# Two layers of a fused graph network: ScalarE's one-hot casts behind the link copies, and layer two's row products three slots ahead

## The chip, the cores and the metric

The kernel runs on one core of one Trainium2 chip. The metric is the device time of one launch in microseconds, as the median of several runs. Three runs of the kernel before took 2488.91, 2496.96 and 2488.14 us; the median is 2488.91.

## What is computed

Three graph attention layers over 3125 nodes with 256 features and 53,125 edges sorted by destination, with a residual and a layer norm behind the second and behind the third. The first two layers have four heads and one head; the third has eight and adds edge features to the scores. The first two add one more loop from each node to itself. Cut to what matters:

```python
def gat_layer(x, src, dst, W, a_src, a_dst, bias, heads, out_ch):
    xW = (x @ W).reshape(n, heads, out_ch)
    alpha_s, alpha_d = jnp.sum(xW * a_src, axis=-1), jnp.sum(xW * a_dst, axis=-1)
    e = leaky_relu(alpha_s[src] + alpha_d[dst], 0.2)
    m = segment_max(e, dst)
    w = jnp.exp(e - m[dst])
    alpha = w / segment_sum(w, dst)[dst]
    return segment_sum(xW[src] * alpha[:, :, None], dst).reshape(n, -1) + bias

h = elu(gat_layer(x, ...,  heads=4, out_ch=64))       # layer one
x = layernorm(x + gat_layer(h, ..., heads=1, out_ch=256))   # layer two
x = layernorm(x + third_layer(x, edge_attr_3, ..., heads=8, out_ch=32))   # layer three
```

## The kernel before

**Batches and slots.** The sorted edges are cut into tiles of 128. A tile that touches two blocks of 128 nodes counts twice, so there are 440 slots; a batch is 11 slots (`B`), and each layer runs 40 batches (`K`). The program is written out batch after batch by `batches(eng, period)`; each engine has its own `period(t, left)` that goes through the slots s = 0 to 10 of batch t and, between them, does pieces of the work for later batches: for the next (`n1`), the one after (`n2`) and the third (`n3`). Each layer's table `AT` says at which slot which piece stands; it is the order of the work, written by hand. Engines meet only by semaphores, and each works its own list strictly in order.

**The work of one batch.** The names are those of the code; the lines are of the profile.

- GpSimd (POOL) fetches the rows of the source nodes with one indirect DMA a slot (L1271) into `rows`, a ring of three batches. The fetches of batch t+3 reuse the buffers of batch t, so slots 0 to 3 wait until the sum of slot 3 of batch t is done, slots 4 to 7 for the sum of slot 7, slots 8 to 10 for the last.
- VectorE makes `onehotT`, the one-hot form of each tile's destinations (`hot`, L716). TensorE transposes it, slots 0 to 5 as group 0 and 6 to 10 as group 1, into banks 0 and 7 (`hot` on PE, L1696, at slots `hotP`). ScalarE casts each group to the float tile `onehot` (`hotT` on ScalarE, L1433, at the two slots `AT[l]["hotT"]`): 128x768 and 128x640. These are the casts of the change. They wait for the transposes and for the sums of the batch two before.
- Scores: TensorE fetches the destination terms (`adst`, L1709), VectorE adds (`scores`, L730 to L742), TensorE transposes (`scoresT`, L1726), ScalarE copies (`scores`, L1440), VectorE scans for the maximum of each segment in both directions (`tops`, L758, `tops2`, L766).
- Links across slots: TensorE turns the ends of the rows (`endsT`, L1735 to L1739), VectorE scans them (`links`, L776, L778, L785), ScalarE copies them to `linkrow` (`link`, L1449, L1450) and computes the factor for older sums (`rescale`, L1457, L1460), TensorE turns the copies to columns (`cols`, L1746) and the factor (L1755), VectorE finishes the maxima (`finish_tops`, L792 to L800).
- Weights: ScalarE takes the exponential (`expw`, L1466), VectorE masks (L808), TensorE transposes (`weightsT`, L1763, L1766), ScalarE copies the weights to `wgt` (L1472, L1474).
- Row products: each slot's rows are multiplied by its weights, on VectorE (L828) or on ScalarE (L1481, one instruction a head), as `OWNER` says. In layer one ScalarE has slots 0, 2, 3, 5, 6, 8 and 9; in layer two all but slot 0. An engine makes the product of slot s + `LEAD[l]` at slot s, running over into the next batch.
- Sums: TensorE multiplies `onehot` with the products (`sum_slot`, L1775, two passes a slot), and VectorE adds the result into `sums` (`add`, L839), after rescaling (L820) at the start of a batch.

**The order around the change.** On TensorE, slot s of the first two layers is the sum of slot s, and behind it the pieces of that slot: in layer one the one-hot groups at 1 and 2, ends at 2, columns at 4, destination terms at 6, weights at 7, scores at 9; in layer two one-hot groups at 0 and 1, ends at 1, columns at 4, destination terms at 5, weights at 7, scores at 8. On ScalarE a slot is written so:

```python
for s in range(B):
    if left > 1:
        if s == AT[l]["link"]:
            link(n1)
            rescale(n1)
        ...
    if s + LEAD[l] in OWN[l]["A"]:
        mul(t, s + LEAD[l])
    if left > 1 and s + LEAD[l] - B in OWN[l]["A"]:
        mul(n1, s + LEAD[l] - B)
    if left > 2 and s in AT[l]["hotT"]:
        hotT(n2, AT[l]["hotT"].index(s))
```

Of the kernel before, what the change touches and what calls it, by code (L numbers as in the profile page):

```python
# [63 lines left out]

OWNER = ("AVAAVAAVAAV", "VAAAAAAAAAA", "VAVAPAPAPAP")
OWN = tuple({e: tuple(s for s in range(B) if o[s] == e) for e in "VAP"} for o in OWNER)
LEAD = (3, 2, 2)
TROW = 8
XPART = 4
PAIRS = (BLOCKS + 1) // 2  # L70
# [13 lines left out]

AT = (
    dict(tops2=1, links=3, finish=5, mask=6, scores=7, tops=10, hot=4, load=5,
         link=5, exp=7, weights=8, hotT=(3, 4), copy=8,
         endsT=2, cols=4, weightsT=7, hotP=(1, 2), adst=6, scoresT=9),
    dict(tops2=0, links=1, finish=5, mask=6, scores=7, tops=10, hot=3, load=8,
         link=2, exp=7, weights=7, hotT=(0, 1), copy=7,  # L90
         endsT=1, cols=4, weightsT=7, hotP=(0, 1), adst=5, scoresT=8),
    dict(links=2, finish=5, mask=10, scores=5, tops=10, hot=7, load=7,
         link=3, exp=6, weights=8, hotT=(2, 6), copy=9,
# [23 lines left out]
def gat_kernel(nc, x, src, dst, edge_attr, w1, as1, ad1, b1, w2, as2, ad2, b2, w3, as3, ad3, edge_w, edge_b, b3, out):  # L117
    ctx = ExitStack()
    with ctx:
# [292 lines left out]
        def _(dve):  # L412
# [247 lines left out]
            for l in range(3):  # L660
# [142 lines left out]
                def mask(t, l=l, H=H):  # L803

                    kk = l * K + t.k
                    R = H * B
                    need(dve, "exp", kk + 1)
                    done(v.tensor_tensor(expT[0:R, 1, :], expT[0:R, 1, :], flags[0:R, t.u, START, :], ALU.mult),  # L808
                         "mask")
# [13 lines left out]
                def mul(t, s, l=l, H=H, V=V):  # L823
                    need(dve, "w", l * K + t.k + 1)
                    n = V - 1 if SELF[l] else V
                    r = rows[:, t.u, s, 0:H * V].rearrange("p (h c) -> p h c", h=H)[:, :, 0:n]
                    w = wgt[:, t.u, 0:H * B].rearrange("p (h s) -> p h s", h=H)[:, :, s:s + 1]
                    done(v.tensor_tensor(r, r, w.to_broadcast([P, H, n]), ALU.mult), "mulv")  # L828
# [67 lines left out]
                def period(t, left, l=l):  # L896
# [5 lines left out]
                    for s in range(B):  # L902
                        if l == 2 and left > 2 and s == AT[l]["tops"]:
                            tops(n2)
                        if left > 1:
# [6 lines left out]
                            if s == AT[l]["mask"] and SELF[l]:  # L912
                                mask(n1)
                        if s + LEAD[l] in OWN[l]["V"]:
                            mul(t, s + LEAD[l])
                        if left > 1 and s + LEAD[l] - B in OWN[l]["V"]:
                            mul(n1, s + LEAD[l] - B)
                        if s == AT[l]["hot"]:
# [41 lines left out]
                def dots_of(t, *groups):  # L960
                    for i in groups:
                        dot(t, i)
                        dot2(t, i)
# [16 lines left out]
                else:  # L980
# [20 lines left out]
                    dots_of(t1, 3)  # L1001
                for s in range(LEAD[l]):
                    if s in OWN[l]["V"]:
# [333 lines left out]
        def _(act):  # L1337
# [68 lines left out]
            for l in range(3):  # L1406
# [69 lines left out]
                def mul(t, s, l=l, H=H, V=V):  # L1476
                    need(act, "w", l * K + t.k + 1)
                    n = V - 1 if SELF[l] else V
                    for h in range(H):
                        r = rows[:, t.u, s, h * V:h * V + n]  # L1480
                        i = a.activation(r, r, ACT.Copy, scale=wgt[:, t.u, h * B + s:h * B + s + 1])  # L1481
                    done(i, "mula")

                def encode(t, i):
                    n = t.k * G + i
                    w = (FACES[i][1] - FACES[i][0]) * D
                    need(act, "facep", n + 1)
                    need(act, "dot", n - 1)
                    done(a.activation(prod[:, i % 2, 0:w], ps_enc[:, 0:w], ACT.Relu), "enc")  # L1489

                def period(t, left, l=l):
                    n1, n2 = t.after(1), t.after(2)
                    plan = faces(t.k) if l == 2 else []
                    for s in range(B):
# [10 lines left out]
                        for p, k, i in plan:  # L1505
                            if p == s:
                                encode(Batch(k // RING, k % RING), i)
                        if s + LEAD[l] in OWN[l]["A"]:
                            mul(t, s + LEAD[l])
# [398 lines left out]
```

How the kernel before makes its waits and increments, by code:

```python
        def need(eng, name, count):  # L324
            if isinstance(count, int) and count <= 0:
                return
            eng.wait_ge(ev[name], count + SEED)
# [1 line left out]
        def need_apart(eng, *waits):  # L330
            for w, c in waits:
                if isinstance(w, str):
                    need(eng, w, c)
                else:
                    eng.wait_ge(w, c)
# [6 lines left out]
        def done(inst, name):  # L344
            return inst.then_inc(ev[name], 1)
# [14 lines left out]
        def table_written(eng, l):  # L360
            for u in range(TROW):
                eng.wait_ge(s_tab[l][u], 16 * len(range(u, BLOCKS, TROW)))
# [47 lines left out]
        @block.vector  # L411
# [7 lines left out]
            def ch(inst):  # L419
                step[0] += 1
                inst.then_inc(p_dve, 1)
                dve.wait_ge(p_dve, step[0])
                return step[0]
# [11 lines left out]
            def products(l):
                H = HEADS[l]
                dve.wait_ge(s_avec[l], 32)
                for i in range(2):
                    ch(v.tensor_tensor(wprod, wts[l][:, :, 0:D],
                                       avec[l][:, i, :].unsqueeze(1).to_broadcast([P, 2, D]), ALU.mult))
                    ch(v.tensor_reduce(wts[l][:, :, D + i * H:D + (i + 1) * H],
                                       wprod.rearrange("p c (h n) -> p c h n", h=H), AX.X, ALU.add))
            dve.wait_ge(s_dst, 48)
            ch(v.tensor_scalar(dst_allf, dst_all, FAR, None, ALU.subtract))
            dve.wait_ge(p_pool, 6)
            for i, e in enumerate((0, TILES - 1)):
```

## Time and profile before

| what | value |
|---|---|
| three runs | 2488.14, 2488.91, 2496.96 us |
| span of the profiled execution | 2493.9 us |
| busy: PE, VectorE, ScalarE, GpSimd | 71%, 64%, 55%, 60% |
| mean granted TensorE clock | 0.770 |
| rescales of layer one (40) | 117.2 to 760.3 us |
| rescales of layer two (40) | 870.8 to 1531.4 us |
| rescales of layer three (40) | 1666.1 to 2456.1 us |

The profile shows one execution. Of its own time, the span is what the profiler saw from the first to the last instruction; nothing else of that execution is listed, and the span lies within the times of the three runs. In a time line a row is an instruction, or several alike in a run (x), with its start from the span's start, its duration, and in brackets the idle time of its engine before it with what ended that. PE is TensorE's matmul, whose ends are modelled, PEld its weight load. "remote" stands where the profile found no instruction whose end fits; "issue" where the engine waited for nothing that the profile shows.

### The profile page before, as it was taken

What the parts mean: (1) busy time and instruction counts of PE and PEld (TensorE: products, weight loads), DVE (VectorE), ACT (ScalarE), POOL (GpSimd) and SP (SyncE); (2) the same over time, 40 slices, a digit from 0 to 9 for tenths busy, and PEclk for the clock granted to TensorE, in tenths of its full rate; (3) what the DMA queues carried; (4) which work ended last, traced back from release to release, by engine and by line L of the source; (5) the groups of instructions that cost most, each with busy time, mean ns of one, the idle gap of its engine ahead of it and who ended that gap; (6) DMA issues with size and microseconds to landing.
All of it is one profiled execution on the core that took longest, in us unless ns stands there. A gap on an engine that the chain in (4) does not pass through costs nothing. (4 is left out here: it accounts for less than half of the span.)

```text
span 2493.9 us, 43223 instructions
## 1 busy us (share of the span) xinstructions
PE 1779.5 (71%) x9241; PEld 1123.8 (45%) x9241; DVE 1586.0 (64%) x4409; ACT 1366.9 (55%) x5004; POOL 1504.0 (60%) x1648
## 2 busy tenths in 40 slices
PE   6267767676766277776776767558888887878874
PEld 5144445444444144444444444335555555555542
DVE  4466666666668155555554556657777777877777
ACT  3255565556556144334344446536676667767666
POOL 3666666666657556656656663626666666766663
PEclk9576676767678566667777677768999989989886
DMA  6644444445531334434433531323433433433331
GB/s 175 160 124 121 115 122 123 118 117 156 144 84 58 97 105 109 111 106 110 112 106 110 164 101 37 113 59 100 114 108 109 117 112 107 114 107 108 107 89 52
DMA packets 130635, 274.39 MB, mean 110 GB/s; under 512 B 39700, under 2 KB 65273, under 8 KB 130366
## 3 DMA queue, kind: packets, MB, share of 16 engines
q0 software_dynamic: 64128, 181.33, 26.9%
q1 hardware_dynamic: 61564, 86.45, 11.6%
q10 hardware_dynamic: 4699, 3.86, 0.6%
q8 instruction: 92, 1.51, 0.2%
q14 instruction: 152, 1.25, 0.2%
HBM read 255.00 MB, written 17.20 MB: 109 GB/s over the span
## 5 line engine op out<-in xcount | busy, mean ns | idle before, releaser
L1271 POOL DMA_INDIRECT rows<-table,index_all x1320 | 1287.8, 976 | 833.2 <-PE bank L1775 383.8
L1775 PE MATMUL bank<-rows,onehot 128*128 128x264 f32 (+1 forms) x2640 | 1089.8, 529 | 290.1 <-ACT rows L1481 156.3
L839 DVE TENSOR_TENSOR sums<-sums,bank 128x264 f32 (+1 forms) x1320 | 555.7, 421 | 465.8 <-PE bank L1775 202.8
L1481 ACT ACTIVATE rows<-rows,wgt 128x33 f32<-128x33 f32 (+2 forms) x3120 | 809.6, 344 | 1.2 <-issue 1.1
L1775 PEld LDWEIGHTS bank<-rows,onehot 128*128 128x128 f32 x2640 | 557.9, 247 | 461.7 <-issue 204.7
L1433 ACT CAST onehot<-bank 128x768 f32<-128x768 bf16 x240 | 177.7, 742 | 301.5 <-remote 174.4
L1489 ACT ACTIVATE prod<-bank 128x512 f32<-128x512 f32 x240 | 133.6, 557 | 244.5 <-PE bank L1787 126.2
L1794 PE MATMUL bank<-late,onehotT 128*128 x1320 | 202.1, 291 | 1.1 <-DVE prod L848 1.1
L848 DVE TENSOR_TENSOR prod<-prod,bank 128x512 f32<-128x512 f32 x240 | 152.4, 635 | 50.3 <-remote 27.4
L857 DVE TENSOR_REDUCE dots<-prod 128x16 f32<-128x512 f32 x240 | 151.7, 632 | 0.5
L1696 PE MATMUL bank<-identb,onehotT 128*128 128x128 bf16 x1320 | 138.3, 251 | 16.6 <-issue 10.0
L1794 PEld LDWEIGHTS bank<-late,onehotT 128*128 128x128 bf16 x1320 | 115.5, 102 | 71.0 <-issue 51.2
L1440 ACT COPY scoreT<-bank 44x256 f32<-44x256 f32 (+2 forms) x120 | 39.2, 327 | 191.1 <-issue 82.5
L828 DVE TENSOR_TENSOR rows<-rows,wgt 128x260 f32<-128x260 f32 (+2 forms) x280 | 120.0, 429 | 35.6 <-ACT wgt L1474 35.6
L1746 PE MATMUL bank<-ones,linkrow 1*44 1x1 f32 (+2 forms) x480 | 47.2, 198 | 130.5 <-ACT linkrow L1450 127.8
L1696 PEld LDWEIGHTS bank<-identb,onehotT 128*128 128x128 bf16 x1320 | 107.7, 114 | 46.7 <-issue 29.2
L1472 ACT COPY rows<-bank 128x44 f32<-128x44 f32 (+1 forms) x80 | 16.4, 205 | 200.0 <-PE bank L1766 159.9
L1746 PEld LDWEIGHTS bank<-ones,linkrow 1*44 1x44 f32 (+2 forms) x480 | 36.6, 140 | 187.3 <-ACT linkrow L1450 160.0
L776 DVE TENSOR_TENSOR_SCAN runs<-chain,bank 1x48 f32<-1x48 f32 (+2 forms) x120 | 29.4, 245 | 142.9 <-remote 139.6
L1283 POOL TENSOR_TENSOR rows<-rows,wgt 128x264 f32<-128x264 f32 x160 | 97.3, 643 | 30.7 <-ACT wgt L1474 30.1
L1787 PE MATMUL bank<-edgew,late 30*128 30x256 bf16 x440 | 96.3, 294 | 14.1 <-ACT prod L1489 8.4
L1726 PE MATMUL bank<-ident,score 128*44 128x128 f32 (+1 forms) x160 | 41.2, 351 | 87.0 <-DVE score L742 69.4
(208 smaller groups left out, 2018.0 us busy)
## 6 DMA issues: line engine op xcount, KB each, us to landing
locb<-loc_d SPq DMA_DIRECT2D x120, 352.0 KB
rows<-table,index_all POOLq DMA_INDIRECT x1320
flags<-flags_d SPq DMA_DIRECT2D x508, 27.5 KB
table<-rows SPq DMA_DIRECT2D x25, 136.0 KB, 1.8
table<-rows SPq DMA_DIRECT2D x25, 134.0 KB
late<-table SPq DMA_DIRECT2D x1, 3300.0 KB
table<-rows SPq DMA_DIRECT2D x25, 129.5 KB, 2.3
late<-table SPq DMA_DIRECT2D x1, 3212.5 KB
```

The source lines that it names most:

```text
L828: done(v.tensor_tensor(r, r, w.to_broadcast([P, H, n]), ALU.mult), "mulv")
L839: done(v.tensor_tensor(a, a, sum_bank(l, t, s)[:, 0:VV], ALU.add), "add")
L848: done(v.tensor_tensor(prod[:, i % 2, 0:w], prod[:, i % 2, 0:w], ps_hdst[i % 2][:, 0:w], ALU.mult), "prod")
L857: done(v.tensor_reduce(dots[:, t.u, :, lo:hi].rearrange("p h s -> p s h"), prod[:, i % 2, 0:(hi - lo) * D].rearrange("p (s h c) -> p s h c ...
L1271: g.indirect_dma_start(out=rows[:, t.u, s, 0:ROW[l]], out_offset=None, in_=table[l], in_offset=bass.IndirectOffsetOnAxis(ap=index_all[:, t ...
L1283: done(g.tensor_tensor(r, r, w.to_broadcast([P, H, n]), ALU.mult), "mulp")
L1433: done(a.copy(onehot[:, t.u, lo:hi, :].rearrange("p s e -> p (s e)"), ps_hotb[l][g][:, 0:(hi - lo) * P]), "hotT")
L1481: i = a.activation(r, r, ACT.Copy, scale=wgt[:, t.u, h * B + s:h * B + s + 1])
L1489: done(a.activation(prod[:, i % 2, 0:w], ps_enc[:, 0:w], ACT.Relu), "enc")
L1696: r = m.transpose(ps_hotb[l][g][:, (s - lo) * P:(s - lo + 1) * P], onehotT[:, t.u, s * P:(s + 1) * P], identb[:, :])
L1775: done(m.matmul(sum_bank(l, t, s)[:, 0:VV], onehot[:, t.u, s, :], rows[:, t.u, s, 0:VV], start=True, stop=True), "agg")
L1794: r = m.matmul(ps_hdst[i % 2][:, (s - lo) * D:(s - lo + 1) * D], onehotT[:, t.u, s * P:(s + 1) * P], hnode3[:, bass.ds(b, 1), j, :].rearra ...
```

## The change

Three numbers of the tables change. In layer one (`AT[0]`) the casts go from slots 3 and 4 to 5 and 6, with the link copies at slot 5. In layer two (`AT[1]`) they go from slots 0 and 1 to 3 and 5, with the link copies at slot 2; and `LEAD[1]` goes from 2 to 3, so that each row product of layer two is made three slots before its sum, on ScalarE and, for slot 0, on VectorE. Layer three is as it was. TensorE, GpSimd and SyncE keep their order to the last instruction.

```diff
-LEAD = (3, 2, 2)
+LEAD = (3, 3, 2)
...
     dict(tops2=1, links=3, finish=5, mask=6, scores=7, tops=10, hot=4, load=5,
-         link=5, exp=7, weights=8, hotT=(3, 4), copy=8,
+         link=5, exp=7, weights=8, hotT=(5, 6), copy=8,
...
     dict(tops2=0, links=1, finish=5, mask=6, scores=7, tops=10, hot=3, load=8,
-         link=2, exp=7, weights=7, hotT=(0, 1), copy=7,
+         link=2, exp=7, weights=7, hotT=(3, 5), copy=7,
```

ScalarE's list in layer two, one batch from the copy of the scores on, before. L1481 with 128x257 is a row product, one a slot (x4 is four slots); L1433 are the casts:

```order
L1440 COPY scoreT<-bank 11x256
L1481 ACTIVATE rows<-rows,wgt 128x257 x4
L1433 CAST onehot<-bank 128x768
L1481 ACTIVATE rows<-rows,wgt 128x257
L1433 CAST onehot<-bank 128x640
L1449 COPY linkrow<-runs 1x11
L1450 COPY linkrow<-runs 1x10
L1457 ACTIVATE rise<-drop 1x1
L1460 ACTIVATE scale<-rise 1x1
L1481 ACTIVATE rows<-rows,wgt 128x257 x5
L1466 ACTIVATE expT<-expT 11x256
```

The same piece of the changed kernel:

```order
L1440 COPY scoreT<-bank 11x256
L1481 ACTIVATE rows<-rows,wgt 128x257 x5
L1449 COPY linkrow<-runs 1x11
L1450 COPY linkrow<-runs 1x10
L1457 ACTIVATE rise<-drop 1x1
L1460 ACTIVATE scale<-rise 1x1
L1481 ACTIVATE rows<-rows,wgt 128x257 x2
L1433 CAST onehot<-bank 128x768
L1481 ACTIVATE rows<-rows,wgt 128x257 x2
L1433 CAST onehot<-bank 128x640
L1481 ACTIVATE rows<-rows,wgt 128x257
L1466 ACTIVATE expT<-expT 11x256
```

Both casts moved from ahead of the link copies to between them and the exponential. Before, the five products ahead of the link copies are those of slots 9 and 10, 1, 2 and 3, and the five behind them those of slots 4 to 8; now they are 10, 1, 2, 3 and 4, and 5 to 9.

ScalarE's list in layer one, one batch, before. L1481 with 128x65 is one head of a row product, four a slot:

```order
L1481 ACTIVATE rows<-rows,wgt 128x65 x20
L1433 CAST onehot<-bank 128x768
L1433 CAST onehot<-bank 128x640
L1449 COPY linkrow<-runs 1x44
L1450 COPY linkrow<-runs 1x4x10
L1457 ACTIVATE rise<-drop 1x4
L1460 ACTIVATE scale<-rise 1x4
L1481 ACTIVATE rows<-rows,wgt 128x65 x8
L1466 ACTIVATE expT<-expT 44x256
```

The same piece of the changed kernel:

```order
L1481 ACTIVATE rows<-rows,wgt 128x65 x20
L1449 COPY linkrow<-runs 1x44
L1450 COPY linkrow<-runs 1x4x10
L1457 ACTIVATE rise<-drop 1x4
L1460 ACTIVATE scale<-rise 1x4
L1481 ACTIVATE rows<-rows,wgt 128x65 x4
L1433 CAST onehot<-bank 128x768
L1481 ACTIVATE rows<-rows,wgt 128x65 x4
L1433 CAST onehot<-bank 128x640
L1466 ACTIVATE expT<-expT 44x256
```

The casts moved behind the link copies here too; the products, of slots 0, 2, 3, 5 and 6 ahead of the copies and of 8 and 9 behind them, stay on their sides.

VectorE's list in layer two, around the register load L868 at slot 8; L828 is the row product of slot 0, L839 an addition into the sums:

```order
-L868 TENSOR_LOAD blk
-L839 ISA
-L839 TENSOR_TENSOR sums<-sums,bank 128x258
 L828 TENSOR_TENSOR rows<-rows,wgt 128x257
+L868 TENSOR_LOAD blk
+L839 ISA
+L839 TENSOR_TENSOR sums<-sums,bank 128x258
```

The product went ahead of the load and of slot 8's addition.

## Rows read from the trace of the kernel before

**Rows 1.** Busy time by stretch, layers one and two: us, busy (instructions), PE clock, DMA share.
```profile
117.00:760.00 643.00, 459.15 (x2236) 300.81 (x2235) 407.58 (x1231) 380.77 (x1473) 408.33 (x420) 0.72 0.44 121
870.00:1531.00 661.00, 480.69 (x2241) 293.59 (x2239) 340.70 (x1089) 274.27 (x783) 388.25 (x411) 0.70 0.39 108
```

**Rows 2.** Waits in layer two: who waited for what, us, times, longest.
```profile
PE bank L1775 <- ACT rows L1481: 146.6, 74, 4.0
POOL rows L1271 <- PE bank L1775: 129.3, 62, 13.9
```

**Rows 3.** Time line, VectorE, layer two: start, us, instruction, idle before, releaser.
```profile
1301.20 0.17 DVE L776 TENSOR_TENSOR_SCAN runs<-chain,bank 1x12 f32<-1x12 f32 x1 [3.42 <-remote]
...
1318.47 0.17 DVE L776 TENSOR_TENSOR_SCAN runs<-chain,bank 1x12 f32<-1x12 f32 x1 [3.18 <-remote]
```

**Rows 4.** Line 820, layer two: the rescale of every batch.
```profile
L820 DVE TENSOR_TENSOR sums<-sums,bank x39: 423/424/426, 870.8 to 1519.1; 128x258 f32 x39
```

**Rows 5.** Time line, TensorE, layer two.
```profile
1302.94 1.23 PE L1775 MATMUL bank<-rows,onehot 128*128 128x258 f32 x2 [2.96 <-ACT rows L1481]
1304.10 0.25 PE L1746 MATMUL bank<-ones,linkrow 1*11 1x1 f32 x4
...
1308.15 0.28 PE L1763 MATMUL bank<-ident,expT 11*128 11x11 f32 x1
...
1315.97 0.17 PE L1739 MATMUL bank<-ident,top 11*1 11x11 f32 x1
...
1316.36 1.09 PE L1775 MATMUL bank<-rows,onehot 128*128 128x258 f32 x4
```

**Rows 6.** Time line, ScalarE, layer two.
```profile
1301.27 0.69 ACT L1433 CAST onehot<-bank 128x640 f32<-128x640 bf16 x1 [2.58 <-remote]
1301.85 0.19 ACT L1449 COPY linkrow<-runs 1x11 f32<-1x11 f32 x1
...
1302.39 2.09 ACT L1481 ACTIVATE rows<-rows,wgt 128x257 f32<-128x257 f32 x5
1305.85 0.42 ACT L1466 ACTIVATE expT<-expT 11x256 f32<-11x256 f32 x1 [1.37 <-DVE expT L800]
```

**Rows 7.** Time line, GpSimd, layer two.
```profile
1301.59 0.94 POOL L1271 DMA_INDIRECT rows<-table,index_all  x1 [1.91 <-PE bank L1775]
...
1305.33 0.95 POOL L1271 DMA_INDIRECT rows<-table,index_all  x1 [0.30 <-issue]
1308.49 0.94 POOL L1271 DMA_INDIRECT rows<-table,index_all  x1 [2.21 <-PE bank L1775]
...
1316.10 0.95 POOL L1271 DMA_INDIRECT rows<-table,index_all  x1 [0.30 <-issue]
```

**Rows 8.** Busy time by stretch around one end of the wait, layer two.
```profile
1317.50:1318.40 0.90, 0.00 (x0) 0.00 (x0) 0.00 (x0) 0.00 (x0) 0.00 (x0) 1.00 0.57 143
1318.40:1319.40 1.00, 0.00 (x0) 0.00 (x0) 0.70 (x4) 0.86 (x4) 0.54 (x1) 0.87 0.03 4
```

**Rows 9.** Time line, VectorE, last batch of layer two.
```profile
1520.33 0.17 DVE L776 TENSOR_TENSOR_SCAN runs<-chain,bank 1x12 f32<-1x12 f32 x1 [0.18 <-PE bank L1739]
```

**Rows 10.** Line 1433, layer two: the one-hot casts.
```profile
L1433 ACT CAST onehot<-bank x76: 692/745/799, 871.2 to 1506.8; 128x768 f32<-128x768 bf16 x38, 128x640 f32<-128x640 bf16 x38
```

**Rows 11.** Time line, ScalarE, one batch of layer one.
```profile
620.30 0.69 ACT L1433 CAST onehot<-bank 128x640 f32<-128x640 bf16 x1 [2.60 <-remote]
620.89 0.22 ACT L1449 COPY linkrow<-runs 1x44 f32<-1x44 f32 x1
...
621.49 2.01 ACT L1481 ACTIVATE rows<-rows,wgt 128x65 f32<-128x65 f32 x8
623.71 0.42 ACT L1466 ACTIVATE expT<-expT 44x256 f32<-44x256 f32 x1 [0.21 <-DVE expT L800]
```

**Rows 12.** Time line, VectorE and GpSimd, the same batch.
```profile
625.20 0.28 DVE L808 TENSOR_TENSOR expT<-expT,flags 44x128 f32<-44x128 f32 x1
...
626.64 0.94 POOL L1271 DMA_INDIRECT rows<-table,index_all  x1 [0.89 <-PE bank L1775]
```

## The prediction

> **What bounds the kernel now.** First the busy time by layer [rows 1]: in the first two layers no engine is busy for more than 0.73 of the stretch (PE 481 of 661 us in layer two). So neither layer is limited by an engine's work, and the question is which waits close the loop from one batch to the next. The waits of layer two [rows 2] name two: PE waited 146.6 us for ScalarE's row products, and POOL waited 129.3 us for PE's sums, with which the buffers for the next gathers come free.
>
> Then one batch of layer two, engine by engine. From one link scan on VectorE to the next it takes 1318.47 - 1301.20 = 17.27 us [rows 3]; over the whole layer, the 39 rescales lie between 870.8 and 1519.1 us [rows 4], that is 648.3 / 38 = 17.06 us.
>
> TensorE issues the sums of slots 2 and 3 at 1316.36 and then stops, since slot 4 needs a product that ScalarE hasn't made: in the batch shown this wait ends at 1302.94 after 2.96 us idle, and ScalarE ends it [rows 5]. ScalarE's row for the same moment [rows 6]: the second one-hot cast starts at 1301.27 after 2.58 us idle, and behind it in the queue stand the link copies (1301.85) and the products from slot 4 on (1302.39). Only then do sum 4, the link columns (1304.10), three more sums and, right behind sum 7, the transposes of the weights (1308.15) follow on TensorE. POOL's fifth gather, which waits for sum 7, starts at 1308.49 after 2.21 us idle [rows 7].
>
> The cast waits for the second group of one-hot transposes, and that is late for a reason of its own. TensorE shows the last transpose of the ends at 1315.97 to 1316.14 [rows 5], yet the scan of the links starts at 1318.47, after 3.18 us idle [rows 3]. The DMA queues are busy for 0.57 up to 1318.4 and for 0.03 just after [rows 8]; POOL's last gather of the batch was issued at 1316.10 [rows 7]. I read this so: behind the one-hot transposes TensorE's completions are held until the gathers' packets have run out. Why, the trace doesn't show. In the layer's last batch, with neither one-hot transposes nor gathers, the scan starts after 0.18 us idle [rows 9]. Call this the hold.
>
> **The change, layer two.** Two edits act as one. Products run three slots ahead, so slot 4's is made before the link copies, in time that ScalarE idles before the hold's end; and the casts go behind the link copies.
>
> - The scans start at 1301.20, so the copies can start near 1301.57, 0.28 us earlier, and with sum 4 issued ahead of the hold the link columns follow near 1302.0 instead of 1304.10: 2.1 us earlier.
> - ScalarE then has five products and both casts before the exponential: 2.09 us [rows 6] and 2 x 0.745 = 1.49 us [rows 10]. From 1302.11 (the products' 1302.39 less 0.28) that is 1305.7; the exponential started at 1305.85 before, waiting for VectorE. It gains at most 0.2 us: ScalarE takes VectorE's place there.
> - The product of slot 7 now stands behind two products and a cast: 1302.11 + 3 x 0.42 + 0.75 = 1304.1. TensorE itself comes later: from the columns to the end of sum 7 it took 1308.15 - 1304.10 = 4.05, now from 1302.0 to 1306.1. So sum 7 is ready 2 us earlier, and POOL's fifth gather can follow the fourth: of its 2.21 us all but the usual gap of 0.30 can go, 1.9 us.
> - What is late next is POOL's stream. Four gathers from 1301.59 to 1305.33 make 1.25 us each; eleven make 13.75, less the last gap of 0.30 is 13.45. From the last one's end (1316.10 + 0.95) to the scan at 1318.47 it is 1.42, and from a scan to the first gather 1301.59 - 1301.20 = 0.39. Sum 15.26 us. The loop through the weights isn't longer: their transposes now wait for exponential and mask, near 1306.8 instead of 1308.15, and gain 1.3 us.
> - I take 15.5 us a batch, 0.24 above that floor, since sum 7 arrives about when the gathers want it: 38 x (17.06 - 15.5) = **59 us less**. Bounds: the floor gives 68; the exponential's 0.2 us alone gives 8.
> - VectorE's product of slot 0 goes ahead of a register load and one addition. The same instructions, that addition 0.42 us later; its weights have been read by the scores just before, so no wait is added. Nothing is added or removed anywhere, DMAs included; SP's and POOL's queues keep their order.
>
> **Layer one.** The link copy stands behind the same cast, and PE's link columns wait for it. But here the cast starts at 620.30 and the copy at 620.89 [rows 11], when the scans had just ended: the copies gain about 0.25 us. Against that, ScalarE finished the products of slots 8 and 9 (2.01 us from 621.49) just in time for the exponential at 623.71. With two casts among them it is free at 623.50 + 1.49 - 0.25 = 624.74, so the exponential starts 1.0 us later and ends at 625.2. The mask that needs it started at 625.20 [rows 12]: the delay is used up to within 0.1 us there. POOL's fifth gather starts at 626.64 after 0.89 us idle, 0.59 over its usual gap. Bounds: a gain of 0.59 us a batch (38 times, 22 us) if the earlier columns reach that wait, a loss of 1.0 us (38 us) if the exponential's delay passes through. I take a gain of 0.1, near the mask's row: **4 us less**.
>
> **Sum.** 63 us less on an execution whose span is 2493.9, so 2431 there; the median of the runs shown, 2488.9, is 5.0 below it, so **2426 us**.
>
> A rule of the Trainium skill speaks against my reading of the hold. The page "SBUF — State Buffer", section "Who interferes with whom", says that DMA never contends with a compute engine, its ports being its own, and that TensorE waits on nobody. In this trace the hold's end and the packets' end coincide [rows 3, 8]; by the rule that is chance. What this would make of the time is the first rival.
>
> **Rivals.**
>
> 1. The hold is TensorE's own, of fixed length from its transposes on, 2.33 us here (1316.14 to 1318.47). The last batch doesn't decide it, since both causes are absent there. Against: rows 8. Then no tail of packets has to be waited for, and all that follows the columns moves by their 2.1 us: 38 x 2.1 = 80, and the 4 of layer one: 2405. That is where the skill's rule leads; chance 0.08.
> 2. Sum 7 is made in time but its completion is held until the fourth gather's packets have run, as in layer one, where POOL idles 0.89 us at that place [rows 12]. Then the fifth gather starts near 1307.6 instead of 1308.49. 38 x 0.9 = 34 less and nothing in layer one: 2455. Chance 0.2.
> 3. ScalarE takes the place of the waits: exponential, mask and weights keep their times, and the batch follows the weights and not the gathers. 0.2 us a batch, 8 us: 2481, within the 0.5% (12.4 us) that a measurement can tell from no change. Chance 0.1.
> 4. Slower. In layer one the exponential is 1.0 us late; if the mask waits for it and VectorE's chain behind the mask sets the batch, all of it passes, 38 us, and with layer two as in the third rival the kernel takes 2519. It decides from about 0.1 us of delay, since the mask has no more slack. Against: in layer one too the batch turns on the hold; the cast there idles 2.60 us until it ends [rows 11], longer than the delay. Chance 0.07.
> 5. The change doesn't do what it says, if the casts came too late for the sums two batches on. They have a whole batch of 16 us to spare, so this gets no chance of its own.
>
> **How the numbers follow.** The forecast, 2410 to 2440, has 0.55; the four rivals 0.08, 0.2, 0.1 and 0.07. The range reaches from 2400, under the first rival (both upper bounds, 68 and 22, give 2399), to 2466, over the second; outside are the last two, 0.17. Faster by over 0.5% is 0.55 + 0.08 + 0.2 = 0.83, the same 0.1, slower 0.07.
>
> **What would show it.** In layer two of the changed kernel: sums 2, 3 and 4 in one run on TensorE; its wait for ScalarE's products, 146.6 us before, nearly gone, and a wait of some 2 us a batch for the link copies in its place; POOL's wait for the sums down from 129 to about 60 us, with the fifth gather one usual gap behind the fourth; 39 rescales over about 590 us; the exponential right behind a product on ScalarE, in both layers. In layer one a batch that is unchanged within 0.3 us. Wrong would be a batch of layer two over 16.5 us, a fifth gather that still idles over 1 us, or a mask in layer one that starts later against the scans than now.

## The result and the profile after

The changed kernel takes 2463.06 us (median of five runs, 2462.12 to 2473.99); the kernel before took 2488.91 beside it. The ratio is 0.9888, with a 95% interval of 0.9862 to 0.9914: 26 us less, where 63 were forecast. The profiled execution of the changed kernel has a span of 2472.2 us, against 2493.9. It was the slowest of the five, 10.9 us above their median.

By stretches: from the first to the last rescale layer two takes 632.9 us where it took 660.6 (27.7 less), and layer one 651.9 where it took 643.1 (8.8 more, see experiment 4). First layer two. These are the rescales and the waits, the lines that answer to [rows 4] and [rows 2] (here all 40 rescales; the kernel before has 870.8 to 1531.4 for them).

```profile
L820 DVE TENSOR_TENSOR sums<-sums,bank x40: 423/424/425, 882.7 to 1515.6; 128x258 f32 x40
```

```profile
POOL rows L1271 <- PE bank L1775: 110.9, 63, 13.0
...
POOL rows L1271 <- remote: 20.2, 12, 2.4
PE bank L1775 <- ACT rows L1481: 8.6, 10, 2.5
```

The wait of TensorE for ScalarE's products is gone, 146.6 us to 8.6. GpSimd's waits shrank far less, 129.3 to 110.9. Some of GpSimd's waits for sums (12 here, 15 before) are ended by a "remote" event, where the profile finds no instruction; with those the sum is 131.1 us, before 156.7 (129.3 and 27.4). The 25.6 us between them are nearly the 27.7 us of the layer. That is the first thing to see: the layer became shorter by little else than what GpSimd waits less.

One batch of layer two in the time line of the changed kernel, from scan to scan (start, us, instruction, idle before and its end):

```profile
1327.76 1.78 PE L1775 MATMUL bank<-rows,onehot 128*128 128x258 f32 x6
...
1330.34 0.17 DVE L776 TENSOR_TENSOR_SCAN runs<-chain,bank 1x12 f32<-1x12 f32 x1 [3.63 <-remote]
...
1330.73 0.94 POOL L1271 DMA_INDIRECT rows<-table,index_all  x1 [1.88 <-PE bank L1775]
...
1330.97 0.24 PE L1746 MATMUL bank<-ones,linkrow 1*11 1x1 f32 x4 [1.44 <-ACT linkrow L1450]
...
1332.76 0.88 PE L1709 MATMUL bank<-dtab,onehotT 128*128 x11
...
1333.57 2.06 PE L1775 MATMUL bank<-rows,onehot 128*128 128x258 f32 x4
...
1334.48 0.95 POOL L1271 DMA_INDIRECT rows<-table,index_all  x1 [0.30 <-issue]
...
1334.62 0.41 ACT L1466 ACTIVATE expT<-expT 11x256 f32<-11x256 f32 x1
...
1335.56 0.28 PE L1763 MATMUL bank<-ident,expT 11*128 11x11 f32 x1
...
1336.56 0.18 ACT L1472 COPY rows<-bank 128x11 f32<-128x11 f32 x1 [1.52 <-PE bank L1766]
1336.58 0.42 DVE L839 TENSOR_TENSOR sums<-sums,bank 128x258 f32 x1 [1.24 <-PE bank L1775]
...
1336.75 0.94 POOL L1271 DMA_INDIRECT rows<-table,index_all  x1 [1.32 <-PE bank L1775]
...
1344.27 0.94 POOL L1271 DMA_INDIRECT rows<-table,index_all  x1 [0.30 <-issue]
1346.71 0.17 DVE L776 TENSOR_TENSOR_SCAN runs<-chain,bank 1x12 f32<-1x12 f32 x1 [3.99 <-remote]
```

The edits do what they say. Sums 2, 3 and 4 stand in one run (x6, two matmuls each), the link columns follow 0.63 us behind the scan (before 2.90), and the transposes of the weights, behind sum 7, 5.22 us behind it (before 6.95). But look at 1336.56 to 1336.75. ScalarE waits for the weights' transposes, VectorE for a sum, GpSimd for sum 7: three different instructions of TensorE, and all three waits end within 0.19 us, some 1 us behind the end of the fourth gather (1334.48 + 0.95 = 1335.43). Sum 7 was issued before 1335.6, yet the fifth gather idles 1.32 us, not 0.30. The batch is 16.37 us.

Is the sum late, or only the word of it? The profile models the ends of matmuls, so its durations can't say, but the trace also records semaphore updates, though not all of them. At the end of the wait for which VectorE's scan is idle above, the update for the transposes of the ends stands at 1330.32, 3.17 us behind their start; where nothing is held it comes 0.18 us behind it. Three sums' updates follow at 1330.43, 1330.47 and 1330.51, though these sums were issued 0.43 us apart. In the whole of layer two, 104 pairs of sums' updates lie less than 0.1 us apart, while no two sums were issued less than 0.43 us apart. So it isn't the matmuls that were late: their completions were held and then let out together.

The batch shown is a usual one. From the fourth batch on, the fifth gather's idle time has a median of 1.37 us, before 2.21. Before, the weights' transposes, right behind sum 7, were mostly issued 0.34 us ahead of that gather; now the median is 1.55 us. In the few batches in which the fifth gather does not wait, the pause tends to come back at the ninth (1.8 to 2.5 us in four batches).

### The profile page after: what moved, and what is told of

It is laid out like the page before. It is cut to its first block and busy times, and to the rows that moved or that the text cites. A ratio compares the mean times of both kernels' runs of the same rounds, so it can differ in the third digit from the quotient of the medians.

```text
span 2472.2 us, 43223 instructions
## 1 busy us (share of the span) xinstructions
PE 1825.0 (74%) x9241; PEld 1149.7 (47%) x9241; DVE 1582.9 (64%) x4409; ACT 1353.8 (55%) x5004; POOL 1504.4 (61%) x1648
## 5 line engine op out<-in xcount | busy, mean ns | idle before, releaser
L1775 PE MATMUL bank<-rows,onehot 128*128 128x264 f32 (+1 forms) x2640 | 1092.5, 530 | 149.7 <-issue 58.5
L839 DVE TENSOR_TENSOR sums<-sums,bank 128x264 f32 (+1 forms) x1320 | 555.6, 421 | 437.8 <-PE bank L1775 214.4
L1481 ACT ACTIVATE rows<-rows,wgt 128x33 f32<-128x33 f32 (+2 forms) x3120 | 817.1, 344 | 1.2 <-issue 1.1
L1775 PEld LDWEIGHTS bank<-rows,onehot 128*128 128x128 f32 x2640 | 566.2, 250 | 323.7 <-issue 208.5
L1449 ACT COPY linkrow<-runs 1x44 f32<-1x44 f32 (+2 forms) x120 | 27.4, 228 | 371.1 <-DVE runs L778 326.8
L1794 PE MATMUL bank<-late,onehotT 128*128 x1320 | 211.4, 300 | 0.7 <-DVE prod L848 0.7
L1433 ACT CAST onehot<-bank 128x768 f32<-128x768 bf16 x240 | 173.9, 726 | 22.7 <-issue 11.5
L1696 PE MATMUL bank<-identb,onehotT 128*128 128x128 bf16 x1320 | 150.9, 267 | 16.1 <-issue 9.8
L1696 PEld LDWEIGHTS bank<-identb,onehotT 128*128 128x128 bf16 x1320 | 117.7, 122 | 50.3 <-issue 32.4
L828 DVE TENSOR_TENSOR rows<-rows,wgt 128x260 f32<-128x260 f32 (+2 forms) x280 | 120.0, 429 | 25.2 <-ACT wgt L1474 25.2
L1709 PEld LDWEIGHTS bank<-dtab,onehotT 128*128 128x128 bf16 x1320 | 90.1, 103 | 48.3 <-issue 20.3
```

Of the source, the lines that this page charges most:

```text
L839: done(v.tensor_tensor(a, a, sum_bank(l, t, s)[:, 0:VV], ALU.add), "add")
L1433: done(a.copy(onehot[:, t.u, lo:hi, :].rearrange("p s e -> p (s e)"), ps_hotb[l][g][:, 0:(hi - lo) * P]), "hotT")
L1696: r = m.transpose(ps_hotb[l][g][:, (s - lo) * P:(s - lo + 1) * P], onehotT[:, t.u, s * P:(s + 1) * P], identb[:, :])
L1775: done(m.matmul(sum_bank(l, t, s)[:, 0:VV], onehot[:, t.u, s, :], rows[:, t.u, s, 0:VV], start=True, stop=True), "agg")
L1794: r = m.matmul(ps_hdst[i % 2][:, (s - lo) * D:(s - lo + 1) * D], onehotT[:, t.u, s * P:(s + 1) * P], hnode3[:, bass.ds(b, 1), j, :].rearra ...
```

## The experiments

Each kernel is given against the kernel before on its own chip. Experiments 1 to 4 share one chip, on which the kernel before takes 2514.9 us; 5 to 8 had 2489.95, 9 to 11 had 2486.12, 12 to 15 had 2489.09. "Batch" is layer two's first to last rescale over 39; "idle" is all that GpSimd waits for sums there ("PE" and "remote" rows) and in how many waits. The times of one chip aren't those of another: layer three, which no experiment touches, takes 796 to 798 us in the traces of 1 to 4 and 780 to 790 us in the others. For 1 to 3 the unchanged layer two is experiment 4's, 16.92 us a batch. Kernels 6, 7, 9 and 10 leave out work (terms, parts of rows, gathers, matmuls), and their output is another.

| kernel | us | ratio [95%] | batch | idle, waits |
|---|---|---|---|---|
| before | 2488.9 | | 16.94 | 156.7, 77 |
| changed | 2463.1 | 0.9888 [0.9862, 0.9914] | 16.23 | 131.1, 75 |
| 1 layer two alone | 2494.4 | 0.9917 [0.9902, 0.9931] | 16.42 | 139.8, 76 |
| 2 casts alone | 2508.5 | 0.9972 [0.9959, 0.9985] | 16.83 | 151.3, 76 |
| 3 products alone | 2494.5 | 0.9910 [0.9895, 0.9925] | 16.43 | 138.6, 74 |
| 4 layer one alone | 2512.4 | 0.9992 [0.9979, 1.0005] | 16.92 | 155.6, 76 |
| 5 transposes with terms | 2461.2 | 0.9882 [0.9841, 0.9923] | 16.29 | 119.3, 71 |
| 6 one term | 2462.0 | 0.9893 [0.9855, 0.9932] | 16.17 | 121.7, 59 |
| 7 narrow rows | 2464.3 | 0.9881 [0.9845, 0.9917] | 16.28 | 131.0, 75 |
| 8 terms earlier | 2471.5 | 0.9927 [0.9899, 0.9956] | 16.28 | 127.5, 76 |
| 9 nine gathers | 2424.9 | 0.9733 [0.9703, 0.9763] | 15.60 | 199.5, 84 |
| 10 few matmuls | 2455.1 | 0.9868 [0.9849, 0.9887] | 16.02 | 112.6, 55 |
| 11 a pause on GpSimd | 2501.4 | 1.0064 [1.0041, 1.0087] | 17.19 | 75.9, 45 |
| 12 one pause, 4 slots | 2485.9 | 0.9997 [0.9974, 1.0020] | 16.79 | 149.7, 74 |
| 13 one pause, 5 slots | 2486.5 | 0.9999 [0.9977, 1.0021] | 16.68 | 134.1, 61 |
| 14 one pause, both layers | 2571.7 | 1.0353 [1.0311, 1.0395] | | |
| 15 changed again | 2468.4 | 0.9924 [0.9897, 0.9951] | 16.29 | 133.8, 79 |

The changed kernel was measured twice, against 2488.9 and, as 15, against 2489.09: 0.9888 and 0.9924. Differences of 0.4% between experiments of different sets are therefore not read as anything.

### 1 to 4: the change taken apart

```
1:  AT[0] hotT=(5, 6) -> (3, 4)
2:  AT[0] hotT=(3, 4); LEAD = (3, 2, 2)
3:  AT[0] hotT=(3, 4); AT[1] hotT=(3, 5) -> (0, 1)
4:  AT[1] hotT=(0, 1); LEAD = (3, 2, 2)
```

> Only the change's layer-two part: casts (3, 5), products three ahead; layer one as before. Theory A: the layer-two part saves 28 us between the first and the last rescale of layer two (16.2 us a batch), and the 13 us that layer one took longer in the changed kernel come from its own casts, so without them they go: 2448 to 2454 us, layer one's rescales over 643 us again. Rival: the longer layer one was chance of that execution, and the time stays near the changed kernel's 2463.

> In layer two only the casts are moved to (3, 5); products stay two slots ahead; layer one as before. Theory A (what counts is when the fourth gather's packets run out, since sum 7's completion is held until then): the casts no longer stand ahead of the link copies, sum 7 is made about 1 us earlier than before, in time for the packets' end, so this half gives nearly all: 16.2 to 16.5 us a batch in layer two, 2450 to 2462 us. Rival: both halves are needed, since slot 4's product still waits behind the link copies; then the batch stays over 16.7 us and the time over 2472.

> In layer two only the products run three slots ahead; the casts stay at (0, 1); layer one as before. Theory A: sum 4 is issued before the hold ends, the link columns come 1.4 us earlier than before, sum 7 is made by the end of the fourth gather's packets, so this half alone too gives nearly all: 16.2 to 16.6 us a batch, 2450 to 2465 us. Rival: the one-hot cast ahead of the link copies delays the columns so far that less than half is gained, over 2475.

> Only layer one's casts moved, (5, 6); layer two as before. Theory A: it costs 9 to 13 us, from the first few batches of the layer, with a steady batch as before (16.4 to 16.9 us): 2496 to 2502 us. Rival, the prediction's own figure: 2485, 4 us less than before.

The products do it: with the lead alone (3) the kernel gains all that both edits gain together (1), and moving the casts alone (2) gives a third. Theory A said that either half would do, and that is refuted for the casts. Layer two of experiment 2 shows why:

```profile
PE bank L1775 <- ACT rows L1481: 123.5, 73, 3.7
```

and of experiment 3:

```profile
PE bank L1775 <- ACT rows L1481: 3.5, 7, 0.8
```

With products two slots ahead slot 4's still stands behind the link copies, whatever else is moved, and TensorE's wait stays (123.5 us of 146.6). In experiment 3 it is 3.5 us, with the casts where they always were: they need no place of their own once sum 4 doesn't wait.

Experiment 4 gives no change that can be measured, 2.5 us less with an interval from -5 to +1. Its profile has a longer layer one (657.1 us from 121.4) than those of 1 to 3 on the same chip (651.2 to 653.1), as the changed kernel's is longer than before, and in both the extra time lies in the first batch. VectorE waits there for a transfer, 7.21 us in experiment 4 and in the changed kernel:

```profile
133.01 0.59 DVE L716 TENSOR_SCALAR onehotT<-locb,pidx 128x1408 bf16<-128x1408 bf16 x1 [7.35 <-DMA locb<-loc_d]
```

It isn't in every execution of the changed kernel. Experiment 15, the same kernel in another execution, has a layer one of 642.4 us (the rescales of line 820, then the same row of the time line, without a wait):

```profile
L820 DVE TENSOR_TENSOR sums<-sums,bank x40: 429/430/430, 119.9 to 762.3; 128x264 f32 x40
```

```profile
123.92 0.58 DVE L716 TENSOR_SCALAR onehotT<-locb,pidx 128x1408 bf16<-128x1408 bf16 x1
```

> The changed kernel itself, on the same chip as the one-pause kernels. If the layer-one part gives nothing: its ratio equals the first experiment's 0.9917 within 0.002. If it gives what the prediction took (4 us): 0.990. If layer one's longer stretch in its profile is real time: 0.994 or more.

0.9924, with 0.9917 for layer two alone: the layer-one part gives nothing that these runs can tell, and the 13 us that theory A charged to it in experiment 1 were read from one execution. The two profiled executions with the wait were 10.9 and 8.2 us above the median of their own kernel, about the size of the wait, so the medians hardly hold it. Whether the change makes it more frequent is open: it is in two of the three traces that have layer one's casts at the new slots and in none of the 14 others, where the longest wait at this place is 0.60 us. The time of experiment 1 accordingly didn't fall below the changed kernel's.

### 5 to 8: what holds the completions, and where

```
5:  AT[1] hotP=(0, 1) -> (5, 6), hotT=(3, 5) -> (8, 9)
6:  adst:   for s in range(B if l != 1 or t.k < 3 else 1):
7:  gather: few = l == 1 and t.k >= RING; w = 64 if few else ROW[l]
8:  AT[1] adst=5 -> 4
(all on experiment 1's kernel)
```

> On the first experiment's kernel (layer two's part alone), layer two's one-hot transposes go from slots 0 and 1 to slots 5 and 6, beside the destination terms, and ScalarE's casts from (3, 5) to (8, 9). Theory A (TensorE's completions behind the one-hot transposes or the destination terms are held until the gathers' packets have run out; two such places in a batch make two drains): one place, one drain. The scans of the links follow the transposes of the ends within 0.5 us, and the gathers of one batch follow those of the last without the 1.8 us between them: about 15.1 us a batch, 50 us less than the first experiment, ratio 0.972. Rival: the transposes delay sum 7 and the weights on TensorE and the batch stays at 16.4, ratio 0.992.

> On the first experiment's kernel: in layer two's batches from the fourth on, the destination terms are made by 1 matmul and not by 11 (10 of the 11 slots' terms are left out, the output is another). Theory A with the matmuls' number as its cause: sum 7's completion comes within 0.3 us of its end, POOL's fifth gather follows the fourth at the usual 0.30 gap, about 15.4 us a batch, ratio 0.976. If the kind and not the number holds the completions (one matmul that reads the transposed one-hot is enough): unchanged, 16.4 us, ratio 0.992.

> On the first experiment's kernel: layer two's gathers from the fourth batch on fetch 64 of the 260 elements of each row (from a packed view of the table, so other values: the output is another); as many gathers, rows and waits. Theory A (the hold ends with the packets): shorter packets, shorter holds; the scans come within 1.0 us of the last gather's end instead of 1.4, the fifth gather waits under 0.6 us, 14.4 to 15.4 us a batch, ratio 0.965 to 0.978. Rival, the prediction's first (the hold is TensorE's own and of fixed length): unchanged, 16.4 us, ratio 0.992.

> On the first experiment's kernel: layer two's destination terms at slot 4, behind the link columns, instead of slot 5. Theory A: sum 7's completion still comes with the end of the fourth gather's packets, whichever sum the terms stand ahead of: within 0.2 us of 16.4 a batch, ratio 0.990 to 0.994. Rival (a hold of fixed length from the terms on): sum 7's completion comes 0.5 us or more earlier, 15.9 us or less, ratio 0.984.

All four came out at 16.2 to 16.3 us a batch, as the layer two of the changed kernel (16.23 and 16.29), which is the same as experiment 1's. For experiment 8 that is what theory A said, and its rival of 15.9 us is refuted. For 5 to 7, read by the totals alone, it looks like three times the rival; the traces say otherwise.

In experiment 5 the hold at the end of the batch did go. The scan runs after 0.18 us of idle time, in the midst of the gathers, as [rows 9] had it with no gathers at all, and no scan of that layer two has a "remote" wait (before: 36 of 39):

```profile
1048.99 0.17 DVE L776 TENSOR_TENSOR_SCAN runs<-chain,bank 1x12 f32<-1x12 f32 x1 [0.18 <-issue]
...
1051.76 0.25 PE L1746 MATMUL bank<-ones,linkrow 1*11 1x1 f32 x4
...
1054.99 0.95 POOL L1271 DMA_INDIRECT rows<-table,index_all  x1 [0.30 <-issue]
1058.12 0.34 DVE L792 SCALAR_TENSOR_TENSOR seg<-flags,bank,top 11x128 f32<-11x128 f32 x1 [3.12 <-remote]
...
1058.78 0.94 POOL L1271 DMA_INDIRECT rows<-table,index_all  x1 [2.85 <-PE bank L1775]
```

The link columns were issued at 1051.76, and VectorE, which needs them at L792, gets them at 1058.12, 2.2 us behind the end of the gather of 1054.99. So the hold only moved to another instruction, one ahead of which no one-hot transpose of this batch stands (they are issued from 1052.88 on): the prediction's "behind the one-hot transposes" was the place, not the cause. Experiment 6 shows the same with one term (the scan at 0.18 us in one batch and 4.56 in the one before), and so the batches alternate, mostly 12 to 14 and 18 to 20 us from rescale to rescale, with the mean unchanged.

Even the same kernel differs in this. A scan is called held where its wait is ended by a "remote" event. These are the waits of the scans in the changed kernel and in experiment 15:

```profile
DVE runs L776 <- remote: 120.7, 33, 4.0
```

```profile
DVE runs L776 <- remote: 84.8, 24, 4.0
```

33 held scans of 39 and 24 of 39, at 16.23 and 16.29 us a batch. In experiment 15 the fifth gather, too, goes through unheld more often (a third of the batches), and the ninth waits about 1.9 us in as many. How often one place is held doesn't set the batch; the pause is taken at another.

Experiment 7 tests the tail of packets. With 64 elements a row the DMA queues rest between one gather and the next and after the last (us, then busy time of the five engines, clock, DMA share, GB/s):

```profile
1020.50:1021.00 0.50, 0.50 (x6) 0.50 (x4) 0.00 (x0) 0.00 (x0) 0.20 (x2) 0.50 0.00 0
1021.00:1021.80 0.80, 0.80 (x3) 0.61 (x3) 0.00 (x0) 0.00 (x0) 0.80 (x1) 0.51 0.22 41
1022.40:1023.00 0.60, 0.40 (x2) 0.00 (x0) 0.00 (x0) 0.00 (x0) 0.00 (x0) 1.00 0.30 55
1023.00:1023.70 0.70, 0.00 (x0) 0.00 (x0) 0.25 (x3) 0.07 (x1) 0.00 (x0) 1.00 0.00 0
```

```profile
1020.92 0.95 POOL L1274 DMA_INDIRECT rows<-table,index_all  x1 [0.30 <-issue]
1023.36 0.17 DVE L776 TENSOR_TENSOR_SCAN runs<-chain,bank 1x12 f32<-1x12 f32 x1 [4.00 <-remote]
```

The scan still comes 1.49 us behind the last gather's end (1.42 before, 1.50 in the changed kernel), although a quarter of the bytes was moved, and at 1020.5 to 1021.0, with the queues at 0.00, nothing came out. So it isn't the amount of transfer. My expectation that shorter rows shorten the hold was wrong: the packets of the last gather end by 1023.0, since they start only 0.6 us or so behind the end of its issue, and the scan comes another 0.36 us later. What this leaves is that completions, once held, come out when GpSimd stops issuing gathers for a while. Here the trace agrees with what the Trainium skill says on the page "SBUF — State Buffer", "Who interferes with whom", that transfers don't contend with a compute engine: a quarter of the bytes leaves the batch at 16.28 us. What the Trainium skill says in the same section, that TensorE waits on nobody, doesn't cover when others hear of its matmuls: by the updates read in the result they heard of them 3 us late.

### 9 to 11: the pauses

```
9:   gather: for s in range(lo, min(hi, B - 2) if l == 1 and t.k >= RING else hi):
10:  adst: as in 6 from t.k 4 on;  hot: for s in range(lo, lo + 1 if l == 1 and t.k >= 4 else hi):
11:  gather, l == 1:  if s == B - 1 and RING <= t.k < K - 3: g.memset(attrT[:, 0:2, :], 1.0)
(all on experiment 1's kernel)
```

> On the first experiment's kernel: in layer two's batches from the fourth on, the gathers of slots 9 and 10 are left out (their buffers keep old rows; the output is another). Theory C (POOL's stream sets the batch: eleven gathers and two pauses, in which it must wait for sums whose completions come only once its gathers have run out): 2 x 1.25 = 2.5 us a batch less, 13.9 us, ratio 0.95 to 0.96. Rival D (another loop of 16.2 us sets the batch and POOL's pauses only fill it up, which would explain why the last four experiments all stayed at 16.2 to 16.3): unchanged, ratio 0.988 to 0.993.

> On the first experiment's kernel: in layer two's batches from the fifth on, one one-hot transpose of each group (of 6 and 5) and one of the 11 destination terms (the others are left out; the output is another). If these matmuls are what starts a hold of TensorE's completions: POOL's pauses shrink from 3.3 to under 1.5 us a batch, 14.7 us or less, ratio 0.965. If the holds start whatever TensorE does beside the gathers: two pauses a batch as before, 16.2 us, ratio 0.988 to 0.993.

> On the first experiment's kernel: in layer two POOL writes a constant over an unused buffer (1 to 2.5 us) ahead of the last gather of each batch. If TensorE's completions are held while gathers are under way and come out when none is: they come out in this pause, the link scans start before the last gather is issued, and the batch grows by at most the pause less 1.2 us. If they are held until the batch's last gather, whatever gap there is: the scans come 1.4 us after the last gather's end as before and the batch grows by the whole pause, ratio 1.01 or more.

Experiment 11 is the plainest:

```profile
1026.87 0.17 PE L1743 MATMUL bank<-ident,top 11*1 11x11 f32 x1
...
1029.56 0.94 POOL L1275 DMA_INDIRECT rows<-table,index_all  x1 [0.31 <-issue]
1030.50 2.46 POOL L1274 MEMSET late<- 30x2816 bf16 x1
1032.52 0.17 DVE L777 TENSOR_TENSOR_SCAN runs<-chain,bank 1x12 f32<-1x12 f32 x1 [6.04 <-remote]
1033.13 0.95 POOL L1275 DMA_INDIRECT rows<-table,index_all  x1 [0.17 <-issue]
```

GpSimd stops gathering for 2.46 us before the last gather, and the scan, in the held batches shown so far behind that gather's end, now comes before its start. In the 34 batches with this pause 14 scans came late (1.3 to 5.5 us behind the transposes of the ends), and all 14 fell within the pause; the others weren't held, but came within 0.2 us. So held completions are let out in a gap of GpSimd's gathers, in the rows shown 1.0 to 2.2 us behind the end of a gather's issue, and not at the end of a batch as such. The batch grows by 0.9 us (17.19 against 16.3) and not by 2.5, since the pause replaces one that was there.

Experiment 9 shows how much GpSimd's stream sets. Two gathers fewer should give 2.5 us a batch if it alone set the batch, and gave 0.7 by the profile (15.60 against the 16.3 of experiments 5 to 8) and 1.0 to 1.2 by the ratio (0.9733 against 0.9888 and 0.9917, over 38 batches). The two differ because the profiled execution, 2440.6 us, is the slowest of four, 15.7 above their median. So the stream bounds the batch only in part: GpSimd now waits 199.5 us for sums, and another bound lies at 15.6 us in this execution, by the ratio at 15.1 to 15.3. Neither theory's number came.

Experiment 10: with 3 of the 22 transposes and terms left, there are 55 pauses in place of 76 and 11 held scans in place of 37, so these matmuls seem to have a share in how often a hold begins, but holds of 5 us and more remain, and 16.02 us a batch. Its ratio of 0.9868 isn't clearly apart from the changed kernel's 0.9888.

### 12 to 14: an order with one pause

```
in each batch of layer two (12, 13) or of one and two (14), with cut = 4, 5, 4:
    part(t.after(2), cut, B)      # gathers slots cut..10, two batches ahead
    part(t.after(3), 0, cut)      # then slots 0..cut-1, three ahead
scores=7 -> 9, scoresT=8 -> 10, copy=7 -> 10
```

> On the first experiment's kernel, layer two's gathers in another order: in each batch POOL first gathers slots 4 to 10 of the batch two ahead and then slots 0 to 3 of the batch three ahead (before: all slots of the batch three ahead), so that all eleven wait only for sums made before the batch begins. Scores and their copies go to slots 9 and 10, since the rows land later. Theory C: one pause instead of two, the fifth gather's wait goes, 15.3 to 15.6 us a batch, 30 to 40 us less than the first experiment, ratio 0.976 to 0.980. Rival: the later rows make the scores late, and with them the link scans; 16.5 us or more, ratio 0.993 or more.

> As one_pause_4, with five slots of the batch three ahead (0 to 4) and six of the batch two ahead (5 to 10). Theory C: sum 4 is now made before the pause too, so this costs nothing more and the rows of the batch two ahead land 1.25 us earlier: 15.3 to 15.6 us a batch, ratio 0.974 to 0.980. Rival: sum 4's completion misses the pause and there are two pauses again: ratio 0.985 to 0.993.

> one_pause_4's order in layers one and two. Theory C: layer one's batch loses its second pause too (1.0 us and more of 16.5), ratio 0.962 to 0.968. Rival: ScalarE and VectorE, which are busier in layer one, take the pause's place there: as one_pause_4, within 0.003.

These were to beat both kernels and didn't: 12 and 13 give back all that the change had gained, 14 loses 3.5%. In 14 the loss is in layer one, whose rescales span 728.8 us in place of 643.0; what it waits for there was not taken apart. In 12 there are two pauses a batch as before, in other places:

```profile
1082.55 0.95 POOL L1277 DMA_INDIRECT rows<-table,index_all  x1 [1.77 <-PE bank L1786]
...
1089.12 0.95 POOL L1277 DMA_INDIRECT rows<-table,index_all  x1 [1.86 <-PE bank L1786]
```

ScalarE's exponential now waits 111.0 us for VectorE between 885 and 1500 us, so this tests the order together with later scores, and theory C isn't confirmed by it: that one pause would give 15.3 us stays unproven. No kernel that does all the work is faster than the changed one by more than the intervals.

## Why the prediction was wrong

The direction was right and so were the places where things move; one term of the sum was not, and it was the largest: 59 us for layer two, where a batch of 16.23 us in place of 16.94 gave 28. The time lies inside the wide range, which reached over the second rival, but one of the prediction's own signs of being wrong came, a fifth gather that still idles over 1 us, and one of its signs of being right did not: GpSimd's wait for sums went to 110.9 us and not to about 60.

- **The wait for ScalarE's products.** Right: 146.6 us to 8.6, sums 2 to 4 in one run, link columns 0.63 us behind the scan (forecast 0.8). In its place I foretold 2 us a batch of waiting for the link copies; it is 1.44 in the batch shown.
- **Sum 7 in time.** Right: the transposes of the weights, behind it, at 5.22 us behind the scan; forecast were sum 7 at 4.9 and these at 5.6.
- **"Of its 2.21 us all but the usual gap of 0.30 can go, 1.9 us."** This step failed. The fifth gather still idles 1.32 us, so 0.89 us went. Over the layer the median went from 2.21 to 1.37 us. Sum 7 was made, but GpSimd isn't told until its first four gathers have run out, and those had been issued in the same time. That is the second rival, in mechanism and nearly in size: 0.9 us a batch, 2455 us; measured 0.71 us over all 39 intervals, 2463. I had given it 0.2. I had seen the hold at the end of the batch and a wait of 0.89 us at the same place in layer one [rows 12], and then treated the first as something that belongs to the transposes instead of to gathers in flight, of which there are some at every place.
- **The floor of 15.26 us.** It counts one pause a batch (1.42 and 0.39 us). Every kernel with eleven gathers kept 16.0 us or more, and with two gathers fewer the batch still took 15.60 in the profiled execution. No run reached the floor.
- **"Behind the one-hot transposes."** As the cause refuted by experiment 5, where the link columns were held. "Until the gathers' packets have run out" fits [rows 8], but in experiment 7 the packets were shorter and the hold ended as far behind the gather's issue as before, and in experiment 11 the queues stood empty for 0.5 us before the scan, so the end of the packets isn't what ends it.
- **Fixed length** (first rival, 2.33 us from the transposes of the ends): refuted. From their end to the scan it is 5.48 us in the batch of experiment 11 (1027.04 to 1032.52), 0.04 us in experiment 5's (1048.95 to 1048.99) and 3.02 us in the changed kernel's.
- **ScalarE takes the place** (third rival): no. Exponential 4.28 us behind the scan, before 4.65.
- **Layer one.** Right as far as it can be told: 4 us forecast, 2.5 us in experiment 4 with zero inside its interval, and nothing between experiments 1 and 15. The exponential does stand right behind a cast and starts later, and the mask absorbs it, as foretold: it starts 4.98 us behind the scan (621.78, scan 616.80), before 4.97 (scan at 620.23, the first row; the others are of the changed kernel).

```profile
620.23 0.24 DVE L776 TENSOR_TENSOR_SCAN runs<-chain,bank 1x48 f32<-1x48 f32 x1 [0.95 <-remote]
```

```profile
616.80 0.23 DVE L776 TENSOR_TENSOR_SCAN runs<-chain,bank 1x48 f32<-1x48 f32 x1
...
620.98 0.41 ACT L1466 ACTIVATE expT<-expT 44x256 f32<-44x256 f32 x1
621.78 0.28 DVE L808 TENSOR_TENSOR expT<-expT,flags 44x128 f32<-44x128 f32 x1
...
622.84 1.17 POOL L1271 DMA_INDIRECT rows<-table,index_all  x1 [1.21 <-PE bank L1775]
```

- **The casts.** I costed both edits as one. The products alone give all of it (0.9910 and 0.9917), and the casts' 1.49 us on ScalarE's path were worth nothing once sum 4 no longer waited.

## What to carry to other kernels

When an engine's wait is to be removed by making its input earlier, ask how the waiting engine learns of it, not only when it is made. If several waits on different instructions of one engine end within 0.2 us of each other, it is likely that none of them was ended by its own instruction: look for what let them all go. And when every reordering moves a wait but no total, count the waits and the time in them over the whole layer: here a pause that left the fifth gather tended to come back at the ninth, and GpSimd kept its 75 to 79 waits in 39 batches.

## What was not expected of the hardware

- While GpSimd issues gathers back to back (0.95 us and a gap of 0.30), completions of TensorE can stay out for up to about 6 us (VectorE idle 6.04 us in experiment 11), and then several come at once, in the rows shown 1.0 to 2.2 us behind the end of the last gather's issue; three sums issued 0.43 us apart were reported within 0.09 us. Not always: in experiment 6 every other scan goes through after 0.18 us, amid the gathers, and in experiment 5 none is held. What starts a hold, and by which path a gather that is under way keeps a completion back, no run here shows; it is open.
- It doesn't depend on the bytes: a quarter of them leaves 1.49 us where 1.42 to 1.50 were, and 24 held scans, as in experiment 15.
- In one profiled execution of the changed kernel the first batch of layer one waits 7.35 us for a transfer, in another of the same kernel not at all. What brings it about is open. A stretch of one execution that differs by 9 us wanted a second one before it was explained.
